# A batched network of two layers on one core: output rows share a PSUM bank with the values, sums of squares share one with a projection, and that projection is issued earlier

## What is computed

```python
grads = vmap(grad(chunk_loss), in_axes=(None, 0, 0, 0))(mem_ws, keys, lr, values)
momentum = assoc_scan(gm, -grads)
updates = assoc_scan(gd, momentum)
w0 = mem_w0 + updates[0]
w1 = mem_w1 + updates[1]
x = einsum('bhncd,bhnde->bhnce', q, w0)
vals = einsum('bhncd,bhnde->bhnce', silu(x), w1)
vals = rmsnorm(vals) * (mh_gamma + 1.0)
vals = vals * gate
out = vals.transpose(0, 2, 1, 3).reshape(b, n, h * dh) @ w_combine
```

## Time and profile before

| | us |
|---|---|
| median of 3 runs | 1223.92 (1217.32 to 1224.34) |
| the profiled execution | 1218.85, of which the span of the profile is 1217.1 |
| PE (matmul) busy | 1111.9 (91%) |
| PEld (weight load) busy | 921.2 (76%) |
| DVE busy | 755.9 (62%) |
| ACT busy | 678.7 (56%) |
| POOL busy | 563.3 (46%) |

### The profile page before, as it was taken

One profiled execution on the slowest core, in us unless ns is written; L12 is line 12 of the kernel. 1 busy time (PEld: TensorE's weight loads), 2 busy tenths in 40 slices (PEclk: granted clock), 3 DMA queues, 4 the chain that ended last, 5 costly groups with the idle time before them and its releaser, 6 DMA issues. The chain is left out here.

```text
span 1217.1 us, 20255 instructions
## 1 busy us (share of the span) xinstructions
PE 1111.9 (91%) x6649; PEld 921.2 (76%) x6650; DVE 755.9 (62%) x1892; ACT 678.7 (56%) x1369; POOL 563.3 (46%) x571
## 2 busy tenths in 40 slices
PE   4689759899999999999999899998999899999995
PEld 3356547788888888888888788887888788888884
DVE  4488846877665656555555555555555555567885
ACT  4567534566555565555555455554555455555653
POOL 3167753477764444444433444343443344434553
PEclk9789959999999999999999999999999999999998
DMA  9133230000300000000000000000000000002222
GB/s 205 31 92 88 87 112 1 3 19 18 98 23 1 1 16 10 9 10 18 8 9 9 20 9 8 8 9 19 8 9 7 19 9 8 5 3 75 86 86 70
DMA packets 57537, 40.32 MB, mean 33 GB/s; under 512 B 4595, under 2 KB 52061, under 8 KB 57310
## 3 DMA queue, kind: packets, MB, share of 16 engines
q1 hardware_dynamic: 53894, 32.10, 9.8%
q0 software_dynamic: 2304, 4.74, 1.2%
q10 hardware_dynamic: 1248, 2.23, 0.5%
HBM read 21.71 MB, written 15.50 MB: 31 GB/s over the span
## 5 line engine op out<-in xcount | busy, mean ns | idle before, releaser
L1106 DVE TENSOR_TENSOR p_sb<-bank,cf 128x512 f32<-128x512 f32 (+3 forms) x512 | 218.8, 481 | 1.5 <-PE bank L827 1.5
L1287 POOL TENSOR_TENSOR sq_rest<-sq,sq_high 128x450 f32<-128x450 f32 x64 | 67.3, 1052 | 154.3 <-ACT sq_high L996 154.3
L1262 POOL TENSOR_TENSOR qa_low<-qa,qa_high 128x450 fp32r<-128x450 f32 x64 | 75.8, 1184 | 125.2 <-ACT qa_high L983 125.2
L850 PE MATMUL bank<-p_sb,du_t 128*128 128x450 f32 (+3 forms) x512 | 130.9, 399 | 0.0
L850 PE MATMUL bank<-p_sb,err_t 128*128 128x450 f32 (+3 forms) x512 | 128.8, 394 | 0.4 <-DVE p_sb L1106 0.4
L1139 DVE SCALAR_TENSOR_TENSOR acc<-bank,rg,acc 128x128 f32<-128x128 f32 x224 | 62.8, 343 | 84.4 <-POOL rg L1275 84.4
L850 PEld LDWEIGHTS bank<-p_sb,du_t 128*128 128x128 f32 x512 | 82.1, 190 | 43.7 <-issue 29.8
L850 PEld LDWEIGHTS bank<-p_sb,err_t 128*128 128x128 f32 x512 | 87.1, 190 | 37.0 <-issue 22.9
L1291 POOL TENSOR_TENSOR sq_low<-sq_rest,sq_mid 128x450 bf16<-128x450 f32 x64 | 66.5, 1039 | 100.2 <-ACT sq_mid L1013 100.2
L981 ACT COPY qa<-bank 128x450 f32<-128x450 f32 x64 | 34.3, 536 | 123.3 <-PE bank L827 123.3
L1175 DVE SCALAR_TENSOR_TENSOR du<-q_sb,bank 128x512 f32<-128x512 f32 x64 | 44.0, 688 | 92.5 <-PE bank L827 92.5
(11 more groups left out here) (304 smaller groups left out, 3185.5 us busy)
## 6 DMA issues: line engine op xcount, KB each, us to landing
x<-in_L_attn_inputs SPq DMA_DIRECT2D x16, 256.0 KB, 3.2
rows<-sorted_rows SPq DMA_DIRECT2D x40, 64.5 KB, 1.8
sorted_rows<-xl_all SPq DMA_DIRECT2D x1, 2064.0 KB, 14.9
x_rows<-x SPq DMA_DIRECT2D x8, 256.0 KB, 2.4
xn_rows<-xn SPq DMA_DIRECT2D x8, 256.0 KB, 2.4
xl_all<-xl SPq DMA_DIRECT2D x8, 256.0 KB, 3.4
ew<-in_L_ffn_w SPq DMA_DIRECT2D x8, 256.0 KB, 4.3
attn_out<-acc SPq DMA_DIRECT2D x7, 256.0 KB, 2.1
```

Source lines behind the costliest of these rows:

```text
L850: last = pe.matmul(out[:, P * i:QW], rows[:, i, :], p_sb[:, P_COL[i]:P_COL[i] + QW - P * i], start=False, stop=True, skip_group_check=True)
L1106: last = nc.vector.tensor_tensor(dst, src, w, ALU.mult)
L1262: nc.gpsimd.tensor_tensor(parts[1][:], whole[:], parts[0][:], ALU.subtract).then_inc(done, 1)
L1287: nc.gpsimd.tensor_tensor(sq_rest[:], sq[:], sq_3[0][:], ALU.subtract).then_inc(g_rest, 1)
```

## The change

Three edits. The output rows go to VB (the bank of the values) in place of QA, and DVE's addition to `acc` reads them there. The sums of squares go to columns 480 to 483 of QA (`SUMS`), beside the 450 columns of the projection, in place of VB, and `ms` reads them there. The QA projection is issued behind the EB projection, ahead of the second scores and the block's transpose. The waits follow the banks: the QA projection now waits for `v_ms` (the sums of the head two before have been read), and the VB product waits for `v_acc` (the output rows have been read). Nothing is computed otherwise, and no instruction is added or removed.

```diff
--- before.py
+++ after.py
@@ -48,6 +48,7 @@
 
 
 PAR, B2 = HF, HF + 2 + FB
+SUMS = QW + 30
 
 
 class Chain:
@@ -861,6 +862,9 @@
                         project(U, m.w_u, f, 0).then_inc(p_u, 1)
                         pe.wait_ge(a_dt, n)
                         project(EB, m.w_v, f, 0, stop=False)
+                        if not (isinstance(n, int) and n < 2):
+                            pe.wait_ge(v_ms, n - 1)
+                        project(QA, m.w_qk, f, SHIFT).then_inc(p_qa, 1)
                     if s is not None:
                         k = n_of(s)
                         pe.wait_ge(v_xl, k + 1)
@@ -872,15 +876,10 @@
                         pe.wait_ge(a_xs, k + 1)
                         pe.transpose(XB[:, 0:P], m.rows[r][:, 0:D], m.ident[:]).then_inc(p_t, 1)
                     if f is not None:
-                        if isinstance(n, int) and n < 2:
-                            pass
-                        else:
-                            pe.wait_ge(v_acc, n - 1)
-                        project(QA, m.w_qk, f, SHIFT).then_inc(p_qa, 1)
                         pe.wait_ge(g_sl, n + 1)
                         product(EB[:], [w[:] for w in w1], [part[:] for part in s_2[h % 2]], start=False).then_inc(p_e, 1)
                     if s is not None:
-                        pe.wait_ge(v_ms, k)
+                        pe.wait_ge(v_acc, k)
                         pe.wait_ge(a_et, k + 1)
                         product(VB[:, 0:QW], [w[:] for w in w1], [part[:] for part in xs_2])
                         apply(VB, err_t, v_p1, k).then_inc(p_v, 1)
@@ -935,11 +934,11 @@
                     if s is not None:
                         pe.wait_ge(a_v, k + 1)
                         for t, r in enumerate(Q_ROWS):
-                            pe.matmul(QA[0:r, t * P:t * P + P], vals[:, t * P:t * P + r], m.w_out[:, s[1], :], start=True, stop=True)
+                            pe.matmul(VB[0:r, t * P:t * P + P], vals[:, t * P:t * P + r], m.w_out[:, s[1], :], start=True, stop=True)
                         pe.wait_ge(g_lo, k + 1)
                         for t, r in enumerate(Q_ROWS):
                             for j, part in enumerate(sq_3):
-                                last = pe.matmul(VB[0:r, t:t + 1], part[:, t * P:t * P + r], ones[:], start=(j == 0), stop=(j == 2))
+                                last = pe.matmul(QA[0:r, SUMS + t:SUMS + t + 1], part[:, t * P:t * P + r], ones[:], start=(j == 0), stop=(j == 2))
                         last.then_inc(p_o, 1)
                     if x is not None:
                         pe.wait_ge(v_yx, x + 1)
@@ -1117,8 +1116,8 @@
                         l = n_of(z)
                         dve.wait_ge(p_o, l + 1)
                         dve.wait_ge(g_rs, l)
-                        nc.vector.tensor_scalar(ms[:, 0:T - 1], VB[:, 0:T - 1], 1.0 / D, RMS_EPS, ALU.mult, ALU.add)
-                        nc.vector.tensor_scalar(ms[0:Q_LAST, T - 1:T], VB[0:Q_LAST, T - 1:T], 1.0 / D, RMS_EPS, ALU.mult, ALU.add).then_inc(v_ms, 1)
+                        nc.vector.tensor_scalar(ms[:, 0:T - 1], QA[:, SUMS:SUMS + T - 1], 1.0 / D, RMS_EPS, ALU.mult, ALU.add)
+                        nc.vector.tensor_scalar(ms[0:Q_LAST, T - 1:T], QA[0:Q_LAST, SUMS + T - 1:SUMS + T], 1.0 / D, RMS_EPS, ALU.mult, ALU.add).then_inc(v_ms, 1)
                     if f is not None:
                         h, n = f[1], n_of(f)
                     if s is not None:
@@ -1132,7 +1131,7 @@
                         else:
                             dve.wait_ge(v_acc, l)
                         for t, r in enumerate(Q_ROWS):
-                            o, g, sums = QA[0:r, t * P:t * P + P], rg[0:r, t:t + 1], acc[0:r, t, :]
+                            o, g, sums = VB[0:r, t * P:t * P + P], rg[0:r, t:t + 1], acc[0:r, t, :]
                             if z[1] == 0:
                                 last = nc.vector.tensor_scalar(sums, o, g, None, ALU.mult)
                             else:
```

## The result

The changed kernel takes 1194.46 us (median of 5 runs, 1189.44 to 1196.63) against 1223.92 before: ratio 0.9768, 95% interval 0.9742 to 0.9794. The forecast was 1195. The profiled execution took 1189.44 us, with a span of 1187.6.

What follows compares the result with a forecast made beforehand. TensorE, busy 91% of the span, was taken as the bound. Gains 16.7 - 1.0 + 0.1 + 9.9 = 25.7 us gave 1193.2 from the profiled 1218.85, or 1198.2 by the median; forecast 1195, range 1187 to 1212.

Steps and rivals of the forecast that it cites:

- The wait that goes: TensorE's QA projection, in steps with a block, waited for the addition to `acc`; 0.72 us per step would go.
- The wait that takes its place: TensorE's EB product would wait some 0.2 us for `s_low`; the VB product would still start 0.54 us earlier.
- The DVE chain: In steps with a block, `xf` starts 0.32 us later but L1170 gives back 0.65, so the 0.54 gain is kept.
- The bound on the weighing: DVE's weighing overlapped by POOL's `qa_low`: no cost taken; if blocked, 0.50 us lost in each of 31 steps.
- Rival B: POOL's `qa_low` blocks DVE's weighing, leaving a gain of 1 to 11 us, about 1213 us; chance 0.12.
- rival C: TensorE, working denser, is granted a lower clock, with 1235 us at 0.96; chance 0.08, shared with unseen causes.
- First heads: Five block steps with a batch's first head ahead: w4t product waits for `err_low`, losing 0.2 us each, 1.0 in all.
- the regular steps: The 31 ordinary steps with a block, each gaining 0.54 us on TensorE, 16.7 us in all.
- Steps without a block: Waits of the projection and the w4t product go: 0.45 us in each of 22 of the 24 steps, 9.9 us.
- Behind the loop's jump: Three block steps where TensorE comes late by itself and did not wait for `acc`: gain 0.

Runs made afterwards that it cites:

- the split wait: Changed kernel with the EB product's matmuls reordered and only the third waiting for `s_low`: 1193.05 us, ratio 0.9746.

## Why the prediction was right

**The wait that goes.** 0.72 us in a step with a block, read from the earlier trace rows: gone in all of them. The waits by engine show it, and the run with the banks alone shows that the exchange of banks is what removes it; moving the projection without it made the wait longer, 2.1 us by the record where it had been 0.5.

**The wait that takes its place.** Foretold: the EB product at 760.94 on the clock of the earlier trace rows, 3.92 into the step. Measured 3.93. The VB product was put at 4.72 and came at 4.74, the w4t product at 8.42 and came at 8.44. The step went from 16.44 to 15.93 us, 0.51 less where I had 0.54.

**The DVE chain.** `xf` was put at 4.09 and came at 4.10; `qa_low` at 3.95 and came at 3.85, 0.03 ahead of the end recorded for `s_low`; L1170 at 6.72 and came at 6.73, with 0.69 as forecast. That its 0.65 us came back is what kept the whole 0.54: `err_low` ended at 8.03, and 0.65 later it would have held the w4t product past 8.44. The run with `qa_low` made late shows it in part, with 1.14 us for this operation and the w4t product at 8.52. The move was not needed for it, though: with the banks alone it took 0.69 in these steps too.

**The bound on the weighing.** The value taken (nothing) holds: 1.68 us after the change, with `qa_low` over its first 0.6, where the step of the earlier trace rows had this without any overlap, in its timeline of DVE:

```profile
761.11 1.67 DVE L1106 TENSOR_TENSOR p_sb<-bank,cf 128x512 f32<-128x512 f32 x4
```

Rival B falls by that pair. The rule of the Trainium skill ("SBUF — State Buffer", Who interferes with whom) gave the same; this trace agrees, with 1.68 us beside 1.67. The same section of the Trainium skill excepts certain modes of DVE from what it says of one SBUF input, and counts copies and casts among what can enter them and so meet GpSimd. The 0.95 us of `yk_high` with the banks alone agrees with that, and in the prediction I had left it out.

**The rivals' clock.** From 430 to 1054 us the granted clock was 0.99, as from 441 to 1079 before; rival C did not come.

```profile
430.00:1054.00 624.00, 610.21 (x3869) 521.87 (x3869) 341.33 (x890) 354.37 (x722) 261.22 (x266) 0.99 0.04 11
```

**First heads.** A loss of 1.0 us was forecast, 1.2 measured, by the mechanism named: the w4t product waits 0.4 us for `err_low` in each of the five and starts at 9.0 to 9.1 us of the step, 0.2 later than before.

**What was mis-sized.** Two terms, which nearly cancelled: 2.9 us more than put down and 1.6 less. With 0.5 less in the regular steps that is how 26.3 stands against 25.7. So the sum is closer than its parts, and that is luck. The median of 1194.5 against the 1195 is luck too: 1195 was a choice between 1193.2 and 1198.2, and 3 us of the measured difference lie outside the steps.

- Steps without a block were put at 0.45 each, 9.9 us in all; they gave 12.8. I had taken from one step what `acc` and `err_low` held back (0.20 and 0.27) and rounded down. The 0.20 was the record's idle time; by the same measure as in the earlier trace rows, from start to start, the wait for `acc` was longer. In the step that began at 281.90 the w4t product came at 7.94, after the change at 7.30: 0.64, of which 0.37 stand at the VB product already and 0.27 are the wait for `err_low`. The first two steps, for which I had put nothing, gave 1.1 and 0.4. One of these steps went the other way, by 0.8 us (14.60 to 15.38), as its row of the cast shows, from the timeline of the changed kernel:

```profile
293.24 1.16 POOL L1261 TENSOR_TENSOR qa_low<-qa,qa_high 128x450 fp32r<-128x450 f32 x1
293.40 1.16 DVE L1156 CAST yk_high<-y_high 128x256 fp32r<-128x256 f32 x1
...
297.28 0.50 PE L828 MATMUL bank<-err_high,w4t_high 128*128 128x512 f32 x1 [1.38 <-DVE err_low L1171]
```

- Behind the loop's jump I had put 0; the three steps lost 1.6 us. From their start to the block's transpose they took 4.55, 4.52 and 4.67 us before and 6.13, 5.29 and 5.27 after. Take off 0.61 for the projection, which now stands in between, and 1.1 us is left, nearly all of it in the first. There TensorE ran longer at the lower of its two clock levels after the pause of some 4 us. The stretches behind the first of these restarts, before and after (columns as in the earlier trace rows):

```profile
690.40:693.60 3.20, 3.19 (x8) 2.57 (x9) 0.24 (x2) 1.48 (x3) 0.18 (x1) 0.50 0.00 0
```

```profile
673.50:676.50 3.00, 3.00 (x7) 2.42 (x8) 0.00 (x0) 1.30 (x3) 0.00 (x1) 0.50 0.00 0
676.50:678.90 2.40, 2.40 (x8) 2.13 (x8) 0.00 (x0) 1.52 (x3) 1.31 (x2) 0.52 0.00 0
```

The granted clock is 0.50 for 3.2 us before, and 0.50 and 0.52 for 5.4 us after. It does not take the projection's new place to have this: in the three restarts of each kernel the way to the transpose was longer than in its regular steps by 1.4, 1.4 and 1.6 us before, by 2.4, 1.6 and 1.5 after, by 2.7, 1.6 and 1.6 in the changed kernel's repeat, and by 1.3, 2.6 and 1.5 with the banks alone. Why it varies is open, and with one trace of the kernel before it is not shown that the change has a part in it.

The other 0.4 us is the change's doing. From the VB product to the w4t product these steps took 3.70 to 3.71 us before and 3.83 to 3.84 after, because the weight load of `apply` now waits for the weighing, which the later transpose has put back (0.24 and 0.36 us in the second of the three). In a regular step the wait for `s_low` gives the weighing that time; behind the jump there is no such wait. The run with the split wait shows the same 3.85 in regular steps, and with the projection back behind the transpose these three steps have 3.70 to 3.71 again. So the prediction costed the later weighing for the regular steps and left it out here.

## What to carry to other kernels

When a wait is there only because two results share a bank, exchange the banks first, and then place the work by what else its place moves: here the same projection is best early in one kind of step and late in the other. Before a gain on one engine is counted, follow the next engine in line, and look there for operations that overlap another engine's on SBUF and last twice as long as their peers: they come back for nothing when the overlap goes, and bite elsewhere when it moves. A term taken from the record's idle time can be too low (0.20 for 0.37 here); measure from start to start against a step that did not wait.

## What the hardware showed that was not expected

- A DVE cast from SBUF to SBUF (256 columns, one input) took 0.95 and 1.16 us when POOL's `qa_low` was running, 0.28 alone; `yb` 1.37 instead of 0.42; `err_low` 1.53 with POOL's `sq_rest`, instead of 0.68. The DVE operations with one operand in PSUM (`acc`, the weighing) kept their 1.12 and 1.68 in the steps shown.
- It goes the other way too: at the five first heads with a block in the kernel before, `qa_low` started while DVE made these copies, took 1.50 to 1.73 us instead of 1.14, and ended 1.0 us behind the last of them each time.
- A pause of TensorE of 2.1 us in each step was followed, in some steps and not in others, by a stretch at the lower clock level: 18.1 and 19.5 us for the same step, granted 1.00 and 0.91. In the kernel before and the changed one, whose waits in these steps are under 0.8 us but for the loop's jump, the clock stood at 0.99.
- After the loop's jump, a pause of TensorE of 3.6 to 4.2 us, the way to the block's transpose took between 1.3 and 2.7 us longer than in a step without the pause, over 27 restarts in nine traces. In some of them the first matmul still ran fast: 0.50 us at 807.86 in the changed kernel, against 0.79 at 673.49.
